# A block of four stages on one core: third and fourth stage joined in one block, with changes at the start and to the banks

## The reference, cut to what matters

```python
x = x + _layernorm(attn0(_layernorm(x)))   # scores x.x^T over all 512 columns, softmax, times x; 8 batches of 512x512
x = x + _layernorm(ffn0(_layernorm(x)))    # x times the sum of 8 factors, / sqrt(8), + bias
x = x + _layernorm(attn1(_layernorm(x)))   # rms norm, q (8 heads of 64), k and v (2 groups), softmax, @ Wo.T, + its input
x = x + _layernorm(ffn1(_layernorm(x)))    # g = x@gate*gate_s; u = x@up*up_s; (silu(g)*u)@down * down_s; inner width 1408
```

## Time and profile before

| what | us |
|---|---|
| median of 3 runs (lowest, highest) | 1505.0 (1503.97, 1506.63) |
| the profiled execution's own time | 1500.94 |
| its span | 1499.1 |
| PE busy in the span | 1404.1 (94%) |
| DVE, ACT, POOL busy | 1012.7, 799.2, 736.9 |

### The profile page before, as it was taken

The page is one execution under the profiler, slowest core; times in us unless marked ns, Lnnn a source line. Parts: engine busy times, 40 slices in busy tenths (PEclk is TensorE's granted clock), DMA queues, the critical chain, the costliest instruction groups (busy, mean ns, idle before and its releaser), DMA issues.

```text
span 1499.1 us, 20689 instructions
## 1 busy us (share of the span) xinstructions
PE 1404.1 (94%) x6864; PEld 1135.9 (76%) x6864; DVE 1012.7 (68%) x2066; ACT 799.2 (53%) x1550; POOL 736.9 (49%) x1002
## 2 busy tenths in 40 slices
PE   4999999897999999999999998598999999999996
PEld 3888877775778787878787876476888888888884
DVE  5888879858888899899898888455242432424333
ACT  4666656648777777777777767332121322212221
POOL 4788646645546464646364636253433324333241
PEclk9999999999999999999999999799999999999998
DMA  7565133331203030303020121241101011010100
GB/s 207 145 169 127 36 99 113 113 99 43 78 15 106 15 106 15 106 15 101 20 67 26 52 104 57 79 147 50 57 1 57 0 56 56 0 56 0 56 28 29
DMA packets 53517, 101.32 MB, mean 68 GB/s; under 512 B 3761, under 2 KB 4785, under 8 KB 53425
## 3 DMA queue, kind: packets, MB, share of 16 engines
q1 hardware_dynamic: 49728, 92.83, 18.4%
q0 software_dynamic: 3696, 7.34, 2.8%
HBM read 70.79 MB, written 25.17 MB: 64 GB/s over the span
## 4 chain that ended last, share of the span: by engine, by line
PE 74%; DVE 13%; POOL 4%; DMA 3%; issue 3%; ACT 2%; SPq 1%; POOLq 0%; DVEq 0%; ACTq 0%
PE f_inner L58 22%; PE context L1758 13%; PE f_down L2165 11%; PE context L58 6%; PE turned L1793 5%; PE score L58 5%; PE score L860 4%; PE context L1819 2%; PE context L1821 2%; DVE g_ptl L1664 2%; DVE g_neg_max L1648 2%; DVE g_q L1572 1%; PE f_inner L2137 1%; PE turned L870 1%; DVE xt L670 1%
## 5 line engine op out<-in xcount | busy, mean ns | idle before, releaser
L1343 POOL TENSOR_SCALAR g_prob<-g_prob,g_inv_sum 128x512 f32<-128x512 f32 x256 | 177.4, 695 | 269.6 <-DVE g_inv_sum L1653 269.5
L58 PE MATMUL f_inner<-f_xth,f_wh 128*128 128x512 f32 x704 | 280.1, 398 | 4.9 <-ACT f_wh L2031 4.8
L58 PE MATMUL f_inner<-f_xtl,f_wh 128*128 128x512 f32 x704 | 279.3, 397 | 0.0
L2072 DVE SCALAR_TENSOR_TENSOR f_hidden<-f_inner,f_inner_scale,f_silu 128x512 f32<-128x512 f32 x88 | 66.0, 750 | 290.9 <-PE f_inner L58 290.9
L2013 ACT ACTIVATE f_silu<-f_inner,f_inner_scale 128x512 f32<-128x512 f32 x88 | 60.6, 689 | 370.3 <-PE f_inner L58 370.3
L1961 POOL TENSOR_TENSOR f_hl<-f_hidden,f_hh 128x512 fp32r<-128x512 f32 x88 | 127.9, 1454 | 249.9 <-DVE f_hh L2078 249.9
L1466 ACT ACTIVATE g_prob<-score,g_neg_max 128x512 f32<-128x512 f32 x256 | 177.1, 692 | 118.6 <-DVE g_neg_max L1648 115.6
L1648 DVE TENSOR_REDUCE g_neg_max<-score 128x1 f32<-128x512 f32 x256 | 174.6, 682 | 46.6 <-PE score L58 45.3
L1664 DVE TENSOR_TENSOR g_ptl<-turned,g_pth 128x512 fp32r<-128x512 f32 x256 | 173.5, 678 | 16.5 <-ACT g_pth L1513 15.3
L1793 PE MATMUL turned<-identity,g_prob 128*128 128x128 f32 x1024 | 155.0, 274 | 16.1 <-DVE g_ptl L1664 15.9
L1793 PEld LDWEIGHTS turned<-identity,g_prob 128*128 128x128 f32 x1024 | 123.3, 140 | 57.9 <-issue 20.6
(11 more groups left out here) (229 smaller groups left out, 3198.2 us busy)
## 6 DMA issues: line engine op xcount, KB each, us to landing
xt<-x_t SPq DMA_DIRECT2D x16, 512.0 KB, 6.2
x_mixed<-x_resident SPq DMA_DIRECT2D x8, 1024.0 KB, 4.3
x_pair<-x_mixed SPq DMA_DIRECT2D x8, 1024.0 KB, 7.8
g_res<-x_mixed SPq DMA_DIRECT2D x8, 1024.0 KB, 6.2
x_attended<-g_res SPq DMA_DIRECT2D x8, 1024.0 KB, 5.1
x_pair<-x_attended SPq DMA_DIRECT2D x8, 1024.0 KB, 5.7
x_resident<-x SPq DMA_DIRECT2D x7, 1024.0 KB, 11.8
factor_sum<-factors POOLq DMA_DIRECT2D x7, 1024.0 KB, 10.5
```

Source lines behind the costliest of these rows:

```text
L58: last = nc.tensor.matmul(out, lhsT, rhs, start=(n == 0), stop=(n == len(pairs) - 1))
L1343: nc.gpsimd.tensor_scalar(prob[:, at, :], prob[:, at, :], inv_sum[:, at:at + 1], 1.0, ALU.mult, ALU.mult).then_inc(prob_ready, 1)
```

## The change

Five things change.

1. Start of stage one: statistics and scales of batch 0 are made in two halves (tiles 0 and 1, then 2 and 3), and what POOL, ACT and DVE do for batch 1 during batch 0 is ordered anew.
2. Stage three has three `turned` banks, the third from what was the second `output` bank, so all heads' outputs use one bank.
3. The pieces of the weights are all read by the end of batch 6, and the count is made at steps 1 and 4 of batch 7.
4. Batch 7 has h0 to h3 as side work, and these are x of the fourth stage's batch 0, so its turned tiles are written there. The weight tiles 0 and 1 are loaded and split in batch 7, and in its steps 26 to 29 the products of inner tile 0 are made; tiles 1 and 2 follow between the drain steps, tile 3 behind Wo.
5. There is no second block: the class `Gated` holds the fourth stage, its tensors lie over those of stage three that are done with, a weight tile's raw values are loaded where its low part will be, and x of batches 0 and 1 is loaded during batches 6 and 7. The register with the count is loaded, and the branch taken, before step 26 of batch 7.

```diff
-            scales_of(0)
-            scaled_x(0, range(T))
+            for h in range(2):
+                first_scales(h)
+                scaled_x(0, (2 * h, 2 * h + 1))
...
-STEP_PIECES = [(20, 28, 30)] * (B - 1) + [(5, 8, 14, 20)]
+STEP_PIECES = [(20, 26, 28, 30)] * 4 + [(20, 28, 30)] * 3
-LOW_COLUMN, LOW_COUNT = 24, 28
+LOW_COLUMN, LOW_COUNT = 1, 4
+HIGH_WEIGHTS = (12, 13, 15, 17, 21, 24)
+LOW_WEIGHTS = (14, 16, 18, 20, 22, 24)
+INNER_FROM = 26
+TILES_AHEAD = 2
...
-        score, turned, output, side = s.score, s.turned, s.output, s.side
+        score, side, output = s.score, s.side, s.output[0]
+        turned = [s.turned[0], s.turned[1], s.output[1]]
...
+            sp.wait_ge(scored, B * UNITS)
+            gated.load_weights(sp, 2)
+            sp.wait_ge(out_ready, B * HEADS - 1)
+            gated.load_weights(sp, 3)
...
+            step(B, 0, 0, False, True, True)
+            act.wait_ge(gated.scale_loaded, 48)
+            act.wait_ge(ol_ready, B * T + 2)
+            gated.silu_of(act, 0, 0, 0, True)
+            step(B, 0, 1, False, True, True)
+            step(B, 0, 2, False, True, True)
+            step(B, 0, 3, False, True, True)
+            gated.silu_of(act, 0, 0, 1, True)
+            gated.high_tile(act, 2)
+            step(B, 0, 6, False, True, True)
...
-                    if not (first and turn_u < 2):
-                        pe.wait_ge(lo_ready, g - TURN_LAG - 1)
+                    else:
+                        pe.wait_ge(lo_ready, g - TURN_LAG - 2)
...
-                        if not (first and hd < 2):
-                            pe.wait_ge(sum_ready, b * HEADS + hd - 1)
+                        if not (first and hd == 0):
+                            pe.wait_ge(sum_ready, b * HEADS + hd)
...
+            def last_steps(with_lo):
+                halves = (range(0, 2), range(2, 4))
+                for u in range(INNER_FROM, UNITS):
+                    step(B - 1, (B - 1) % 2, u, False, True, False)
+                    if u == INNER_FROM:
+                        pe.wait_ge(side_free, side_use(B, "wo0") - 1)
+                        gated.weights_of(pe, 0, with_lo)
+                    if u == INNER_FROM + 2:
+                        pe.wait_ge(side_free, side_use(B, "wo0"))
+                    if u < INNER_FROM + 4:
+                        gated.inner_part(pe, 0, 0, (u - INNER_FROM) // 2, halves[(u - INNER_FROM) % 2], with_lo)
...
+                gated.weights_of(pe, 2, with_lo)
+                gated.inner_of(pe, 0, 0, 2, with_lo)
                 for t in range(T):
+                    side_share(B, f"wo{t}", 0, 3 * T, True)
+                gated.weights_of(pe, 3, with_lo)
+                gated.inner_of(pe, 0, 0, 3, with_lo)
...
+    def load_weights(self, sp, i):
+        if i >= 4:
+            sp.wait_ge(self.wh_ready, parts_done(i - 4))
+        for j, src in enumerate(self.weights):
+            sp.dma_start(self.raw[i][:, 1, j, :], src[i, :, :]).then_inc(self.raw_loaded[i % 4], 16)
```

More of the change, by code:

```diff
@@ L745, in body @@
                 inverse(b, p, 3)
-                if not last:
+                if not last and not first:
                     lo_of_xn(b + 1, 1 - p, 3)
@@ L1077, in side_runs @@
         return not first
-    return not drain and (not last or name in OWN)
+    return not drain and (not last or name in IN_LAST)
 BY_MAP = sum(MAP_PIECES)
@@ L1684, in step @@
                     low_count()
+                if last and not drain and u in LOW_WEIGHTS:
+                    gated.low_part(dve, LOW_WEIGHTS.index(u) // 3, LOW_WEIGHTS.index(u) % 3)
                 for t in range(T):
@@ L1824, in step @@
                         mm.then_inc(out_ready, 1)
-                for name, start, end, done in side_works(u, first, last, drain):
-                    side_share(b, name, start, end, done)
+                if not drain:
+                    for name, start, end, done in side_works(u, first, last, drain):
+                        side_share(b, name, start, end, done)
             def body(b, p, first, last):
@@ L1887, in gated_ffn @@
-        silu = sb("silu", [P, 2, N])
-        hidden = sb("hidden", [P, 2, N])
-        hh, hl = sb("hh", [P, 2, N], F32R), sb("hl", [P, 2, N], F32R)
-        y = sb("y", [P, T, N])
-        bn, mv, ve, rs, shift = norm_in.bn, norm_in.mv, norm_in.ve, norm_in.rs, norm_in.shift
-        obn, omv = sb("obn", [P, T, 6]), sb("omv", [P, T, 2])
-        ove, ors, oshift = sb("ove", [P, T]), sb("ors", [P, T]), sb("oshift", [P, T])
-        inner = [bank(f"inner{i}") for i in range(4)]
-        down = [bank(f"down{i}") for i in range(T)]
```

860 lines of the change are left out of this document (520 added, 340 removed).

## The result

The changed kernel takes **1460.39 us** in the median (1459.18 to 1461.43, 4 runs) and the one before 1505.55 (1503.97 to 1506.63, 4 runs): 0.9701 of the time, with a 95% interval of 0.9689 to 0.9713. That is 45 us where 36 were forecast, and 1460.4 where the forecast was 1469. It lies outside of the 1464 to 1475 that the main forecast claimed for itself, and just inside the wider 1460 to 1480. The profiled execution took 1460.45 us, with a span of 1458.6; the one of before had a span of 1499.1. So the two traces, which are compared here, differ by 40.5 us, and the other 4.6 is what the profiled execution of before stood under its median. What the record shows of these 4.6 us stands under "the drain", in the part on the prediction.

What follows compares the result with a forecast made beforehand. PE sets the pace, so only its idle or low-clock time can be gained. Seam 31 (26.0 + 2.5 + 2.5), start 2.4, banks 2.5: 36 us off 1505 gives 1469 us, range 1464 to 1475 (0.62), wider 1460 to 1480 (0.82).

Steps and rivals of the forecast that it cites:

- The fourth stage's start: Stage four's first batches: waits of 8.25, 4.81 and 7.15 us and 5.8 us of slow work go, together 26.0 us.
- Work moved into batch 7: Stage three's batch 7: 5.5 us of PE work moved in, less 2 for DVE and 1 for load and branch, net 2.5.
- My 2 us for DVE's load: Batch 7, steps 12 to 24: extra DVE work makes the batch 2 us longer, range 0 to 3.3.
- I take 1, since PE often waits there for DVE: Step 26 of batch 7: register load and taken branch cost 1 us, range 0.5 to 4.8.
- The prediction's rival of the branch: Step 26 of batch 7: branch stalls PE 0.5 to 4.8 us, 4 us more than taken, 1473 us; chance 0.08.
- The drain: End of stage three: tiles 1 and 2 fill PE's waits ahead of Wo, holes from 6.2 to 3.7 us, gain 2.5.
- Tile 2's wait: Drain: PE waits 2.1 us for the high part of tile 2's weights, loaded behind the residual.
- The single output bank: Last two heads of stage three share one output bank: about 1 us; costs nothing in the steady part.
- The start: Start of stage one: PE's wait for batch 1 shrinks, 2.4 us gained, bounds 1 and 4.8.
- Banks: Stage three outside the seam: third turned bank gains 2.5 us (0 to 9.1); the wait mostly changes its name.
- my walk for batch 1's first inner product: Walk through the seam into stage four: batch 1's first inner product at about 1010 instead of 1041.7 us.
- the rival that gave the banks all of their waits: Stage three's turned banks: 9.1 us gained instead of 2.5, time 1462 us; chance 0.12.

Runs made afterwards that it cites:

- before_pad64: The kernel before with 64 empty bytes behind inner_scale and nothing else; 1505.61 us, ratio 1.0007 to the kernel before.
- before_pad160: The kernel before with 160 empty bytes behind inner_scale and nothing else; 1493.47 us, ratio 0.9925 to the kernel before.
- before_new_start: The kernel before with only the change to the start of stage one, nothing of stages three and four; 1502.62 us, 0.9991 of the kernel before.
- after_w01_off: The changed kernel with the weights of tiles 0 and 1 (and wq, wk, wv in the same place) moved down by 32 bytes; 1462.76 us.

## Why the prediction was right, and where not

- *The fourth stage's start* (26.0 us with the low clock): right. From the last `Wo` product to batch 1's first inner product it was 40.1 us less for a forecast of 39, and some 1.3 of these 40.1 are the faster products (an estimate: 216 products at 6.1 ns).
- *Work moved into batch 7.* My 2 us for DVE's load was right: without the branch, batch 7 up to its last score is 1.8 us longer than before. The step that failed is the sentence "I take 1, since PE often waits there for DVE". The branch makes batch 7 3.1 us longer, with 1.2 us of low clock in that, and 1.7 us remain behind the drain. The prediction's rival of the branch, to which it gave 0.08, came true in its mechanism and inside its 0.5 to 4.8 us of length; its price of 4 us was too high. I had put a loop's jump beside it, where PE idles 0.06 us in 210, and taken it for the same case. It isn't: what matters is whether the target's instructions are there, and the arm for weights with low parts lay in between.
- *The drain*: "the drain's holes go from 6.2 us to 3.7: 2.5 us" was wrong. They are now 1.64 + 1.15 + 2.17 + 0.73 = 5.7 us. (The new waits that it named add to 3.1 us and not to 3.7, and the old ones went from 1.35 us, and not from 1.66.) Tile 2's wait was sized right (2.1 for 2.17). The single output bank cost 2.8 us where I had about 1, since I counted it at one head only; and I had no wait for `g_ol`. What I overlooked: the trace of before was a lucky one here. In before_pad64, whose code is that of before but for the pad, the 48 `Wo` products run in part at the low clock, where before had it in full (windows of before, then of before_pad64):

```profile
940.00:945.00 5.00, 5.00 (x23) 4.13 (x22) 2.01 (x7) 0.00 (x0) 1.95 (x5) 1.00 0.00 0
```

```profile
940.00:945.00 5.00, 5.00 (x13) 3.87 (x13) 0.74 (x6) 0.00 (x0) 2.05 (x5) 0.53 0.00 0
```

  Its drain takes 28.4 us instead of 23.4, and its own time, 1505.56 us, is the median of before. The record of granted clocks says the same of before itself: of the 23 executions beside the pads of 32 and 64 bytes, five took 1501.3 to 1501.9 us, at a mean clock of 0.985, and eighteen 1504.1 to 1507.0 us, at 0.980 to 0.982, and none between. So most executions of before have some 4 us of low clock more than the profiled one. That they have them in the drain is shown for before_pad64 alone, and before_pad160 is near its median with a drain of 23.4 us. The changed kernel's four executions lie within 2.3 us, at 0.989 to 0.991. The forecast had let the 4 us between profiled execution and median stand, and the change took them away too: that is 4.6 of the 45 us.
- *The start*: 1.5 us by the medians of before_new_start (interval 0 to 2.7) and by the first pair of traces, 2.4 by the means of all traces, for a forecast of 2.4. The term was right as far as can be told.
- *Banks*: the wait changed its name, as foreseen (7.5 us in 14 pieces for `g_prob`, longest 1.2). 2.5 us were forecast for all. Undone in the changed kernel they cost 3.6 us by the medians (1464.02 to 1460.39, measured at two times), 2.8 in batches 0 to 6 and 1.7 in the seam by the traces. In the comparison of before and after it looks like 1.3, because what else the change does to these batches takes 1.5 back.
- *What was missing*: "what a change brings there is PE's idle time, the time in which PE works at a low clock, or nothing". I took PE busy in all of the time for a fixed pace, and counted products only. 9.7 us came out of that pace. With 1.3 us more of it in the first batch it is 11 us of the 45 between the medians, and of the 40.5 between the traces. Without it the gain would have been 34 or 29.5 us (the one with, the other without the 4.6 us of low clock above), below the forecast of 36, so the forecast came close to the result because terms that were missed made up for terms that were too large. That is luck, and so are two other agreements: the 1010 us of my walk for batch 1's first inner product (1010.86 measured), which left the start and the banks out, and the 1462 us of the rival that gave the banks all of their waits, which did not happen.
- *The signs*: those of being right came (no wait for `f_xn` between the stages, inner products at full clock right behind `Wo`, `g_prob` in the place of `g_ptl`), and so did three of those of being wrong: a wait of over 1 us for tile 2's high part, a hole at step 26, and a batch 7 that was more than 4 us longer.

## What to carry to other kernels

An engine that is busy in all of a window is not yet at its best: compare the number of instructions that fit in the same length of window in two stages or two kernels, and if a change moves buffers, work out where operands come to stand. Here a pad of 160 bytes was worth 11.5 us, where the whole rebuilt seam brought 28 between the two traces. Before a forecast is set against a median, ask what the profiled execution lacks of it, and whether the change takes that away too. Put the arm that is usually taken right behind a branch, above all where work stands ready behind it, and look for a transfer of instructions in a hole whose named releaser had long been done.

## What was not expected of the hardware

Products of 512 columns of fp32r that follow each other start every 0.2267 us where the moving and the stationary operand start at the same byte modulo 256 in their partitions, and every 0.231 to 0.234 us where they don't. A difference of 0 was fast (the changed kernel but for tile 9, and the pads of 160 and 416 bytes). Counted as moving less stationary operand, modulo 256, these were slow: 96 and 160 (inner and down products of the kernel before, and the other way round with 64 bytes), 128 (both, with 32 bytes), 32 and 224 (inner and down products of tiles 0 and 1 in after_w01_off, which start at 17088 beside 41696), 192 and 64 (tile 9). So all multiples of 32 but 0 were met, and all cost 6 to 7 ns a product, save that tile 9's down products, at 64, cost 4. With 128 the two products of a pair had unlike steps, 0.2359 for those reading `xth` and 0.2300 for `xtl`, with the same mean. The weight loads themselves stay at 188 ns in all of these traces. Differences that are no multiple of 32, and what in the memory makes the pattern, were not tried.
